# A gated long-convolution layer on one core: the low half of a split operand is formed from on-chip memory, and its bank goes to the near-lag products

## The reference, cut to what matters

```python
xp = (einsum('btd,de->bte', X, Wp) + bp).reshape(B, T, STAGES + 1, D)   # B=4, T=2048, D=256, STAGES=3
f  = (sine_positional_encoding(T, D) @ Wf + bf).reshape(T, STAGES, D)
y = xp[:, :, 0, :]
for i in range(STAGES):                       # causal convolution with f, then a gate
    y = irfft(rfft(y) * rfft(f[:, i])) * xp[:, :, i + 1, :]
x = layernorm(X + y)
h = silu(x @ wg.T) * (x @ wu.T)               # HIDDEN = 768, int weights / 127
out = layernorm(x + h @ wd.T)
```

## Time and profile before

| | us |
|---|---|
| median of 3 runs | 973.63 (972.66 to 973.94) |
| profiled execution, its own time | 972.62 |
| its span, first to last instruction | 970.4 |
| PE busy | 876.6 (90%) |
| DVE busy | 767.4 (79%) |
| POOL busy | 645.3 (66%) |
| ACT busy | 529.7 (55%) |

### The profile page before, as it was taken

How to read it: one execution, slowest core, us unless ns; L and a number is a source line. 1 busy time by engine, 2 the same in 40 slices (tenths; PEclk the granted TensorE clock), 3 DMA queues, 4 the chain that set the end, 5 groups by cost and what they waited for, 6 DMA issues and landing times. The chain is left out here.

```text
span 970.4 us, 21584 instructions
## 1 busy us (share of the span) xinstructions
PE 876.6 (90%) x8204; PEld 678.0 (70%) x8204; DVE 767.4 (79%) x1318; ACT 529.7 (55%) x1048; POOL 645.3 (66%) x679
## 2 busy tenths in 40 slices
PE   3999999947999999999999999954899999999994
PEld 2888888846888888888888888732456556555563
DVE  2777777735899898888889889846688898988864
ACT  2253334446788888878887667314344444444441
POOL 2555555403888898898898889862676666667642
PEclk8999999969999999999999999996999999999998
DMA  5596556488566567566667877328123224222011
GB/s 205 192 348 214 188 173 205 165 230 238 164 189 174 165 194 197 174 179 175 193 195 213 262 235 209 109 105 276 45 66 120 77 65 130 65 77 74 23 45 44
DMA packets 165788, 155.16 MB, mean 160 GB/s; under 512 B 3457, under 2 KB 151937, under 8 KB 165313
## 3 DMA queue, kind: packets, MB, share of 16 engines
q1 hardware_dynamic: 164176, 145.24, 49.3%
q10 hardware_dynamic: 1520, 8.68, 2.3%
HBM read 111.18 MB, written 42.73 MB: 159 GB/s over the span
## 5 line engine op out<-in xcount | busy, mean ns | idle before, releaser
L564 POOL TENSOR_TENSOR gz<-prod 128x512 f32<-128x512 f32 x180 | 230.4, 1280 | 88.2 <-DVE prod L507 87.0
L507 DVE TENSOR_TENSOR prod<-bank,wfx 128x1024 f32<-128x1024 f32 x180 | 219.8, 1221 | 32.5 <-ACT bank L437 30.7
L396 PE MATMUL bank<-gz,ei 128*128 128x256 f32 x720 | 186.8, 382 | 2.2 <-POOL gz L564 2.0
L149 PE MATMUL bank<-wps,xs 128*128 128x512 f32 x768 | 176.4, 392 | 5.6 <-POOL xs L250 5.6
L149 PEld LDWEIGHTS bank<-wps,xs 128*128 128x128 f32 x768 | 145.6, 190 | 36.1 <-DVE wps L218 5.7
L939 POOL TENSOR_TENSOR hl<-hf,hh 128x512 f16<-128x512 f32 x96 | 111.8, 1173 | 82.4 <-ACT hh L793 82.4
L437 ACT COPY bank<-bank 128x512 f32<-128x512 f32 x180 | 102.8, 571 | 105.4 <-PE bank L344 105.4
L250 POOL TENSOR_TENSOR xs<-xt,xs 128x256 fp32r<-128x256 f32 x128 | 93.3, 752 | 97.4 <-ACT xs L181 97.4
L574 POOL TENSOR_TENSOR y<-y,gate 128x256 f32<-128x256 f32 x192 | 143.3, 747 | 5.1 <-DVE y L518 5.1
L344 PE MATMUL bank<-yh,ef 128*128 128x256 f16 x720 | 137.6, 273 | 2.3 <-ACT bank L437 1.3
L396 PEld LDWEIGHTS bank<-gz,ei 128*128 128x128 f32 x720 | 122.8, 190 | 15.8 <-POOL gz L564 6.5
(11 more groups left out here) (77 smaller groups left out, 1960.2 us busy)
## 6 DMA issues: line engine op xcount, KB each, us to landing
toep<-filter_rows SPq DMA_DIRECT2D x48, 1024.0 KB, 7.1
gates<-staged SPq DMA_DIRECT2D x16, 1536.0 KB, 6.3
gate<-gates SPq DMA_DIRECT2D x48, 512.0 KB, 4.1
xt<-in_XT SPq DMA_DIRECT2D x16, 512.0 KB, 5.0
attn_out<-y SPq DMA_DIRECT2D x16, 512.0 KB, 5.5
ya<-attn_out SPq DMA_DIRECT2D x16, 512.0 KB, 4.6
xr<-in_X SPq DMA_DIRECT2D x16, 512.0 KB, 5.4
out_x<-oo SPq DMA_DIRECT2D x16, 512.0 KB, 3.4
```

The lines of the kernel that those rows point to most:

```text
L149: mm = pe.matmul(bank[n % 4 * 2 + half][:, :], xs[:, n % XSS, half, hx, k, :], wps[:, hw, k, half * 512:(half + 1) * 512], start=(k == 0 a ...
L396: mm = pe.matmul(dst, ei[:, h, e0 * P:(e0 + 1) * P], gz[:, n % 3, h, :], start=False, stop=(h == 1))
L507: nc.vector.tensor_tensor(prod[:, n % 2].rearrange("p r j (c b) -> p r j c b", b=NB), b_copy[n % 2][:, :].rearrange("p (r c b) -> p r c b" ...
L564: nc.gpsimd.tensor_tensor(gz[:, n % 3], prod[:, n % 2, 0], prod[:, n % 2, 1], ALU.add).then_inc(gz_ready, 1)
```

## The change

`b_y` and its ACT instruction go. DVE forms `yl` with one `scalar_tensor_tensor` from `y` (SBUF), the scale and `yh` (SBUF): value times scale, less `yh`. Bank 6 becomes the second near-lag bank: pieces go by turns to banks 0 and 6, and TensorE waits for the write-back of the piece before the last.

```diff
-        b_toep, b_state, b_copy, b_out, b_y, b_pre = bank[0], bank[1], bank[2:4], bank[4:6], bank[6], bank[7]
+        b_toep, b_state, b_copy, b_out, b_pre = (bank[0], bank[6]), bank[1], bank[2:4], bank[4:6], bank[7]
...
-                        if m >= 1:
-                            pe.wait_ge(toep_out, m)
+                        if m >= 2:
+                            pe.wait_ge(toep_out, m - 1)
...
-                        dst = b_toep[:, c * 64:(c + 1) * 64]
+                        dst = b_toep[m % 2][:, c * 64:(c + 1) * 64]
...
-                    if u * NQ + q >= 1:
-                        act.wait_ge(yl_ready, u * NQ + q)
                     cols = slice(q * QW, (q + 1) * QW)
-                    nc.scalar.activation(b_y[:, :].rearrange("p (a w) -> p a w", w=QW), y[:, u % NG, :, cols], ACT.Copy,
-                                         scale=scale(u)).then_inc(ys_ready, 1)
                     nc.scalar.activation(yh[:, u % 2, :, cols], y[:, u % NG, :, cols], ACT.Copy,
                                          scale=scale(u)).then_inc(yh_ready, 1)
...
-                        b_toep[:, :].rearrange("p (c a b) -> p c a b", c=CQ, b=NB), ACT.Copy,
+                        b_toep[m % 2][:, :].rearrange("p (c a b) -> p c a b", c=CQ, b=NB), ACT.Copy,
...
-                    dve.wait_ge(ys_ready, u * NQ + q + 1)
-                    nc.vector.tensor_tensor(
-                        yl[:, u % 2, :, cols], b_y[:, :].rearrange("p (a w) -> p a w", w=QW),
-                        yh[:, u % 2, :, cols], ALU.subtract).then_inc(yl_ready, 1)
+                    nc.vector.scalar_tensor_tensor(
+                        out=yl[:, u % 2, :, cols], in0=y[:, u % NG, :, cols], scalar=scale(u),
+                        in1=yh[:, u % 2, :, cols], op0=ALU.mult, op1=ALU.subtract).then_inc(yl_ready, 1)
```

More of the change, by code:

```diff
@@ L269, in program @@
         scale_ready = sem("scale_ready")
-        ys_ready = sem("ys_ready")
         yh_ready = sem("yh_ready")
```

## The result

The changed kernel takes 981.0 us (median of 5 runs, 978.35 to 982.83), the one before 973.03 (5 runs, 972.45 to 973.94). The ratio is 1.0079, 95% interval 1.006 to 1.0097: 0.8% slower, 8 us where 11.8 were forecast. The profiled execution has a span of 979.2 us, 8.8 more than before.

What follows compares the result with a forecast made beforehand. PE was taken to set the pace, busy 42.41 of 43 us. Terms 11.8 + 0.5 + 0.35 - 0.8 = 11.8 us gave 984.4 profiled, 985.4 median; own range 981 to 992, wider range 976 to 1003.

Steps and rivals of the forecast that it cites:

- Two SBUF inputs on DVE and POOL exclude each other: Seen at `pb`: a DVE instruction with two SBUF inputs and a POOL instruction exclude each other; the first goes first.
- The first unit: `yl(1)` meets a `gz`, ends at 237.81 where PE wants it at 237.50: 0.35 us.
- The last start with a split: Tenth start, without factors: `yl(1)` comes 0.17 us ahead of `gz`, late only through `yl(0)`: 0.5 us.
- A held-up `yl` ends 0.53 us after POOL: Any hindered `yl` of 512 columns, from `pb` ending 0.27 us after POOL for 256 columns.
- that of `yl(0)`: Start of a unit: POOL's apply hinders `yl(0)`, so the next `prod` starts 0.54 us later.
- The nine starts: At nine unit starts `yl(1)`, hindered by `gz`, ends 1.31 us later and PE waits for it: 11.8 us.
- Half the exclusion: Rival: DVE gets in first more often and POOL waits; about 0.5 us a unit, 978 us, chance 0.09.
- Unhindered duration: New `yl` from SBUF without POOL in its way: between 0.62 and 0.68 us, taken as 0.68.
- The cover in the middle of a unit: `gz` still ends 0.5 us ahead of need: 0 counted. Rival, cover gone: 1000 us, chance 0.17.
- ACT's relief: Dropping ACT's copy to bank 6, 96 instructions and 66.8 us of ACT: counted as 0.
- The second bank: Last piece before the first unit no longer waits for ACT's write-back: 0.8 us off, once, bounds 0 and 2.
- The heavier sum: By the shared-port rule a hindered `yl` follows POOL by its whole 0.68 us, not 0.53: 0.15 more each.

Runs made afterwards that it cites:

- psum_read: New `yl` instruction with its first input from PSUM bank 6 (stale values), against the changed kernel with one near-lag bank: 974.81 us, ratio 1.0022 to the kernel before.
- split_pv: `pv` moved to free PSUM bank 6, against the changed kernel with one near-lag bank: 971.99 us, ratio 1.0003 to the kernel before.
- only_q1: Kernel before, ACT's copy and its waits kept, with `yl` from SBUF for piece q = 1 alone: 980.67 us, ratio 1.0081.
- all_but_q1: Kernel before, ACT's copy kept, with `yl` from SBUF for the seven pieces other than q = 1: 973.65 us, ratio 1.0012.
- only_q0: Kernel before, ACT's copy kept, with `yl` from SBUF for piece q = 0 alone: 972.95 us, ratio 1.0001.
- keep_copy: Kernel before with all eight pieces of `yl` from SBUF, but ACT's copy and its waits kept: 979.61 us, ratio 1.0073.

## Why the prediction was right, and where it was off

The direction, the place and the mechanism came out as forecast; the size was off by a third. 981.0 lies on the lower edge of the forecast's own range (981 to 992), and that it does is in part luck: the forecast had one delay too many in each unit, and in the profiled execution some 1 us that can't be shown to be the change's doing went the other way.

- *Two SBUF inputs on DVE and POOL exclude each other, and this holds for the new form.* Shown by psum_read: the same instruction with one input in PSUM is never held up (730 to 753 ns over 96), and POOL's durations go back. split_pv shows it from the other side with `pb`.
- *Where it costs.* At `yl(1)`. only_q1 makes all of the loss and all_but_q1 almost none of it. PE's wait grew by 0.79 us in each of nine places, 7.1 of the 8.8 us of the span; with the 0.05 of `yl(0)` in each, these units are 7.6 us longer. The first unit has 0.44 more (PE waits 0.23 us there), where 0.35 was forecast. The last start with a split has 0.44 more, where 0.5 was forecast, but the second was luck: `yl(0)` delays the next `prod` by only 0.06 there, and what costs most is that `gz` stands aside for `yl(1)` and PE waits 0.26 us for it. The 1.0 us behind the last `prod` is no effect that the change can be shown to have: both kernels run the same instructions there, and this stretch takes 327.6 to 329.8 us in the twelve kept traces. Its granted clock was 0.95 before and 0.94 after.
- *A held-up `yl` ends 0.53 us after POOL.* It was 0.55 to 0.56 where I read it.
- *The term that was mis-sized* is that of `yl(0)`: "New end 301.85 + 0.53 = 302.38 ... so here at 302.42: 0.54 later." It was 0.06 later, from 0.60 to 0.66 between the starts of `yl(0)` and `prod`, and that only since the new form is slower by 0.05 us. The nine starts were sized at 1.31 and measured 0.79; the difference, 9 x 0.52 = 4.7 us, is the error and more; 0.5 us for the slower form and the 1.0 behind the last `prod`, which I hadn't counted, went the other way. The rival *Half the exclusion* named what happened at `yl(0)`: DVE gets in first and POOL bears the wait. Its price of 0.5 us a unit was too low, since `yl(1)` does wait. I took the order of the recorded starts as the order in which the two engines get their turn. only_q0 shows that it is not: 0.16 us behind the apply, `yl(0)` goes first. An explanation that I put into the expectations on the way (`yl(0)` goes first because POOL is late by then) fell with the same run, in which POOL is on time. What decides the turn is still open.
- *Unhindered duration.* I bounded it by 0.62 and 0.68 and took 0.68; it is 0.73. The form, not the memory, makes the difference: 0.74 from PSUM. The estimate from the Trainium skill ("VectorE: DVE Perf Modes", the TRN2 errata), a shorter instruction from SBUF, is not borne out by this pair, where the two sources differ by 0.01 us; the measurement decides. The 0.06 between `pb` and the gather, on which I had the rows agree with it, lies between two forms too: `pb` itself takes 0.42 us from either memory (split_pv).
- *The cover in the middle of a unit holds.* POOL went from 37.54 to 41.01 of 43 us, `gz` from 1280 to 1442 ns, and PE never waited for it there. all_but_q1 shows it by time.
- *ACT's relief is worth nothing.* keep_copy.
- *The second bank.* I took 0.8 us off for the last piece before the first unit; counted from the moment at which the filter blocks are there, the traces have 0.3.
- *The rule of the shared port* ("SBUF — State Buffer", "Who interferes with whom", in the Trainium skill) has the later one blocked for the whole instruction. The trace agrees on the blocking. The heavier sum that I had tied to it did not come: 0.55 us and not the full 0.73 follow POOL's end.

## What to carry to other kernels

Before a DVE operand is moved from PSUM to SBUF, look at what GpSimd does at that moment: a DVE instruction with two SBUF inputs and a GpSimd one took turns here, and what that costs depends on whether anything waits for it. 84 of 96 such instructions cost almost nothing and 12 cost 8 us. A bank that comes free is best given to the operand whose removal from SBUF ends a collision on the path (`pv`: 8 us), not to the one that double-buffers something that almost nobody waits for (0.3 us). And the order of a few short instructions in front of the one that PE waits for was worth 3 us by itself.

## What was not expected

- A POOL instruction let a DVE instruction go first that was recorded 0.16 us later, 10 times out of 10; another held up one recorded 0.06 us later. The order of recorded starts doesn't tell who goes first.
- `scalar_tensor_tensor` with a scalar read from memory took 0.73 to 0.74 us for 512 columns, from SBUF and from PSUM, where `tensor_tensor` with one input in PSUM took 0.68. Whether the scalar or the second operation costs it was not tested.
- `pb` in the kernel before had lost 0.79 us to the same exclusion at 11 of the 12 starts of a unit. The durations of the earlier trace rows told it, and I had read them only as a sign of what `yl` would do, not as time that could be won back.
